# A feed forward with 64-wide inner products: two batches side by side in TensorE's array

## The chip, the cores and the metric

The kernel runs on one core of a Trainium2 chip, in one launch, all in fp32. The metric is the device time of that launch in microseconds (us); "before" is the median of three runs.

## What is computed

The reference is a decoder of four blocks over `x` (4 batches x 256 tokens x 128 features), each an attention over the context and a feed forward, added to `x` through tanh gates. The part that matters here is the feed forward of the second block, a two-layer mixture with low rank R = 64 whose 16 gates come from an entmax:

```python
    def cp_mumoe(x, gate, Win, Wout):
        ones = jnp.ones(x.shape[:-1] + (1,), x.dtype)
        xb = jnp.concatenate([x, ones], axis=-1)
        z = jnp.einsum('btd,dr->btr', xb, Win) * gate
        return jnp.einsum('btr,or->bto', z, Wout)
...
        a = entmax15(layernorm_noaffine(jnp.einsum('btd,de->bte', x, proj)))
        g1 = jnp.einsum('bte,er->btr', a, C1)
        h = cp_mumoe(x, g1, Win1, Wout1)
        h = jax.nn.gelu(h, approximate=False)
        g2 = jnp.einsum('bte,er->btr', a, C2)
        return cp_mumoe(h, g2, Win2, Wout2)
```

Here E = 16 gates, R = 64, D = 128, and the hidden width O = 512. So `C1`, `C2` contract over 16 rows into 64 columns, `Win1` over 128 into 64, `Wout1` over 64 into 512, `Win2` over 512 into 64, and `Wout2` over 64 into 128.

## The kernel before

`x` lies transposed in SBUF, features on the 128 partitions and a batch's 256 tokens along the free dimension. Up to about 1060 us the kernel runs the first block and a long six-layer local attention; then comes `pe_tail`, `act_tail`, `dve_tail` (with small parts in `pool_tail`), which this case is about. Each engine runs its own written-out order of instructions, and semaphores (`s["..."]`) tie them together. In the tail every stage loops over the four batches, and batch b owns the two PSUM banks 2b and 2b + 1 (a bank is 512 fp32 columns per partition).

The stage of this case, by line, is this chain; "product" is one `e.matmul` of the program, which the trace records as two MATMULs:

- Layer norm of `x`: `pe_ln_centre` (L234), square (L239), `pe_ln_var` (L244), Ln and Exp (L249, L251), multiply (L256).
- Router logits (L1289), keys and values of the next attention (L1294, L1296), `Win1` for the four batches (L1301). `IDLE1` = 6 products of 512 columns whose result nobody reads (L1304) keep PE running while DVE computes the entmax (L1615 to L1678).
- `m1_a`: eight transposes turn the gates (L1309), two for each batch.
- Per batch: ACT copies the turned gates (L1517), PE multiplies them by `C1` and `C2` (L1315, L1316), ACT copies both results (L1520), DVE forms `z1` = (Win1 x + bin1) * g1 (L1727).
- Per batch: four products with `Wout1` (L1322), contraction over 64 partitions, 128 columns wide; then two Gelus of 128x512 on ACT (L1523, L1524).
- Per batch: four products with `Win2` accumulate into 64 partitions (L1329); DVE forms `z2` (L1732); `Wout2` (L1335); DVE adds to `x` (L1736).
- The next block begins with the layer norm of `x` (L234 again), then its attention (L1127 and on).

All loops above run over the four batches inside each step, so PE does `Wout1` for all four, then `Win2` for all four, and so on. ACT loads an activation table when the function changes: at L1523 for Gelu by itself, and at L1525, where the program asks for the next one (`preload_act_table_set`).

Other products of the kernel use only a part of the array too: in the fourth block's attention, L1423 contracts over 32 partitions (`rows = slice(32 * (2 * pair + c), ...)`, with c as the innermost loop) and L1437 writes 32 partitions (`out[32 * g:32 * g + 32, :]`, with g as the innermost loop).

Of the kernel before, what the change touches and what calls it, by code (L numbers as in the profile page):

```python
# [10 lines left out]
ALU = mybir.AluOpType  # L11
ACT = mybir.ActivationFunctionType
AX = mybir.AxisListType

B, N, D = 4, 256, 128
P = 128
NT = N // P
BANK = 512
# [10 lines left out]
E1, R1, O1 = 16, 64, 512  # L29
# [45 lines left out]
def split(ap, n):  # L75
    return ap.rearrange("p (n k) -> p n k", n=n)
# [1120 lines left out]
        e.tensor_tensor(p, p, stretch(over, N), ALU.mult).then_inc(s["at_normalised"], 1)  # L1197


HT2_ROWS = [min(P, (E2 + 1) * HID2 - i * P) for i in range(HT2)]  # L1200


# [65 lines left out]
def pe_tail(e, s, m):  # L1268
# [7 lines left out]
    for b in range(B):  # L1276
# [3 lines left out]
                 skip_group_check=True).then_inc(s["mix_made"], 1)  # L1280
# [5 lines left out]
    for b in range(B):  # L1286
        e.wait_ge(s["ln_out"], LN_L1F + b + 1)
        for t in range(NT):
            made = e.matmul(m.bank[2 * b][:, t * E1:(t + 1) * E1], m.xn[b][:, t * P:(t + 1) * P], m.W(7, "proj"),  # L1289
                            start=True, stop=True, skip_group_check=True)  # L1290
        made.then_inc(s["m1_logits"], 1)
    for b in range(B):
        b1 = m.bank[2 * b + 1]
        e.matmul(b1[:, 0:N], m.W(7, "Wk"), m.ctx[b], start=True, stop=True, skip_group_check=True)  # L1294
        for t in range(NT):
            made = e.matmul(b1[:, N + t * P:N + (t + 1) * P], m.ctx[b][:, t * P:(t + 1) * P], m.W(7, "Wv"), start=True,  # L1296
                            stop=True, skip_group_check=True)
        made.then_inc(s["p_made"], 1)
    for b in range(B):
        e.wait_ge(s["p_kept_act"], 8 + b + 1)  # L1300
        e.matmul(m.bank[2 * b + 1][0:R1, 0:N], m.W(7, "Win1"), m.xn[b], start=True, stop=True, skip_group_check=True)  # L1301
    e.wait_ge(s["m1_var"], 1)
    for n in range(IDLE1):
        e.matmul(m.bank[0], m.ident, m.x_all[:, 0:BANK], start=True, stop=True, skip_group_check=True)  # L1304
    e.wait_ge(s["m1_a"], 1)
    for b in range(B):
        for t in range(NT):
            i = b * NT + t
            made = e.transpose(m.bank[2 * b][0:E1, t * P:(t + 1) * P], m.router[7][:, i * E1:(i + 1) * E1], m.ident)  # L1309
        made.then_inc(s["m1_turned"], 1)  # L1310
    for b in range(B):
        b0 = m.bank[2 * b]
        aT = m.t_w[b][0:E1, 0:N]
        e.wait_ge(s["m1_a_kept"], b + 1)
        e.matmul(b0[0:R1, 0:N], m.W(7, "C1")[0:E1, :], aT, start=True, stop=True, skip_group_check=True)  # L1315
        e.matmul(b0[0:R1, N:2 * N], m.W(7, "C2")[0:E1, :], aT, start=True, stop=True,  # L1316
                 skip_group_check=True).then_inc(s["m1_made"], 1)
    for b in range(B):
        z1 = m.t_w[b][0:R1, 2 * BANK:2 * BANK + N]
        e.wait_ge(s["m1_z1"], b + 1)  # L1320
        for o in range(4):
            made = e.matmul(m.bank[2 * b + o // 2][:, o % 2 * N:(o % 2 + 1) * N], m.W(7, "Wout1")[0:R1, o * P:(o + 1) * P],  # L1322
                            z1, start=True, stop=True, skip_group_check=True)
        made.then_inc(s["m1_h"], 1)
    for b in range(B):
        hT = split(m.t_v[b], 4)
        e.wait_ge(s["m1_gelu"], b + 1)
        for o in range(4):
            made = e.matmul(m.bank[2 * b][0:R1, 0:N], m.W(7, "Win2")[:, o * R1:(o + 1) * R1], hT[:, o, :], start=(o == 0),  # L1329
                            stop=(o == 3), skip_group_check=True)  # L1330
        made.then_inc(s["m1_w2"], 1)
    for b in range(B):
        z2 = m.t_w[b][0:R1, 2 * BANK + N:3 * BANK]
        e.wait_ge(s["m1_z2"], b + 1)
        e.matmul(m.bank[2 * b + 1][:, 0:N], m.W(7, "Wout2")[0:R1, :], z2, start=True, stop=True,  # L1335
                 skip_group_check=True).then_inc(s["m1_out"], 1)

    for b in range(B):
        e.wait_ge(s["l1f_done"], b + 1)
# [21 lines left out]
    for step in range(HT2 + LAG2 + 1):  # L1361
        i = step
# [123 lines left out]
def act_tail(e, s, m):  # L1486
# [25 lines left out]
    e.activation(root, delta, ACT.Ln, bias=m.floor).then_inc(s["m1_root"], 1)  # L1512
    e.wait_ge(s["m1_root"], 1)
    e.activation(root, root, ACT.Exp, scale=0.5).then_inc(s["m1_root"], 1)
    for b in range(B):
        e.wait_ge(s["m1_turned"], b + 1)
        e.activation(m.t_w[b][0:E1, 0:N], m.bank[2 * b][0:E1, 0:N], ACT.Copy).then_inc(s["m1_a_kept"], 1)  # L1517
    for b in range(B):
        e.wait_ge(s["m1_made"], b + 1)
        e.activation(m.t_w[b][0:R1, BANK:2 * BANK], m.bank[2 * b][0:R1, :], ACT.Copy).then_inc(s["m1_g"], 1)  # L1520
    for b in range(B):
        e.wait_ge(s["m1_h"], b + 1)
        e.activation(m.t_v[b][:, 0:BANK], m.bank[2 * b][:, :], ACT.Gelu)  # L1523
        e.activation(m.t_v[b][:, BANK:2 * BANK], m.bank[2 * b + 1][:, :], ACT.Gelu).then_inc(s["m1_gelu"], 1)  # L1524
    e.preload_act_table_set("natural_log_exp_and_others")  # L1525
    act_ln4(e, s, m, LN_L2X, m.ln_tail, m.eps)
    act_attention(e, s, m, 2)
# [161 lines left out]
def dve_tail(e, s, m):  # L1689
# [31 lines left out]
    e.wait_ge(s["l1x_done"], B)  # L1721
    dve_ln4(e, s, m, LN_L1F, m.ln_tail, m.xn)
    dve_entmax(e, s, m, link)
    for b in range(B):
        g, z1 = m.t_w[b][0:R1, BANK:2 * BANK], m.t_w[b][0:R1, 2 * BANK:2 * BANK + N]
        e.wait_ge(s["m1_g"], b + 1)
        e.scalar_tensor_tensor(out=z1, in0=m.bank[2 * b + 1][0:R1, 0:N], scalar=m.W(7, "bin1")[0:R1, :], in1=g[:, 0:N],  # L1727
                               op0=ALU.add, op1=ALU.mult).then_inc(s["m1_z1"], 1)
    for b in range(B):
        g, z2 = m.t_w[b][0:R1, BANK:2 * BANK], m.t_w[b][0:R1, 2 * BANK + N:3 * BANK]  # L1730
        e.wait_ge(s["m1_w2"], b + 1)
        e.scalar_tensor_tensor(out=z2, in0=m.bank[2 * b][0:R1, 0:N], scalar=m.W(7, "bin2")[0:R1, :], in1=g[:, N:2 * N],  # L1732
                               op0=ALU.add, op1=ALU.mult).then_inc(s["m1_z2"], 1)
    for b in range(B):
        e.wait_ge(s["m1_out"], b + 1)
        e.scalar_tensor_tensor(out=m.x[b], in0=m.bank[2 * b + 1][:, 0:N], scalar=m.gates[:, B + 1:B + 2], in1=m.x[b],  # L1736
# [286 lines left out]
def chunked(a, rows=P):  # L2023

    n = -(-a.shape[0] // rows)
    full = np.zeros((n * rows,) + a.shape[1:], a.dtype)
    full[:a.shape[0]] = a
    return full.reshape(n, rows, -1).transpose(1, 0, 2).reshape(rows, -1)


def column(a):
    return chunked(a.reshape(-1, 1))
# [6 lines left out]
def layouts(i):  # L2039
# [11 lines left out]
    for d in range(DEPTH):  # L2051
        qs, ks = i["L0_ffn_q_scale"][d], i["L0_ffn_k_scale"][d]
        swap = lambda a: np.concatenate([a[DH // 2:], a[:DH // 2]])
        b1 = i["L0_ffn_b1"][d]
        wqkv = i["L0_ffn_Wqkv"][d]
        wv = wqkv[:, 2 * INNER:].reshape(D, H0, DH)[:, v_order].reshape(D, INNER)
        wo = i["L0_ffn_Wo"][d].reshape(H0, DH, D)[np.array(o_order)].reshape(INNER, D)
        packs.append(packed(L0F, {
            "Wqkv": np.concatenate([wqkv[:, :2 * INNER], wv], 1), "Wo": chunked(wo), "W1": i["L0_ffn_W1"][d],
            "W2": chunked(i["L0_ffn_W2"][d]), "scales": row(np.concatenate([qs, ks, swap(qs), swap(ks)])),  # L2060
            "ln_g": column(i["L0_ffn_ln_g"][d]), "ln_b": column(i["L0_ffn_ln_b"][d]),
            "b1": np.concatenate([column(b1[:FF]), column(b1[FF:])], 1), "b2": column(i["L0_ffn_b2"][d])}))
    one = {}
    for n in ("q_c", "k_s", "v_s", "q_s", "k_c", "v_c"):
        one["W" + n], one["b" + n] = i[f"L1_xattn_W{n}"].T, column(i[f"L1_xattn_b{n}"])
    wg = i["L1_xattn_Wg"].T
    one.update({
        "Wg_a": wg[:D], "Wg_b": wg[D:], "bg": column(i["L1_xattn_bg"]), "proj": i["L1_ffn_proj"],
        "C1": i["L1_ffn_C1"], "C2": i["L1_ffn_C2"], "Win1": i["L1_ffn_Win1"][:D], "bin1": i["L1_ffn_Win1"][D:].T,
        "Wout1": i["L1_ffn_Wout1"].T, "Win2": chunked(i["L1_ffn_Win2"][:O1]), "bin2": i["L1_ffn_Win2"][O1:].T,  # L2070
        "Wout2": i["L1_ffn_Wout2"].T, "gamma": column(i["L2_xattn_gamma"]), "beta": column(i["L2_xattn_beta"])})
    for n in "qkv":
        one["W" + n], one["b" + n] = i["L2_xattn_W" + n], column(i["L2_xattn_b" + n])
    packs.append(packed(MIX1, one))
# [40 lines left out]
```

## Time and profile before

| | us |
|---|---|
| before, median of 3 runs | 1402.86 (1399.28 to 1403.01) |
| the profiled execution, its own time | 1402.63 |
| its span (first to last instruction) | 1400.8 |
| TensorE busy in the span | 1272.3 (91%) |
| VectorE / ScalarE / GpSimdE busy | 980.5 / 934.2 / 741.9 |
| mean granted TensorE clock | 0.963 of full |

The profile is of one execution, and all instants below are microseconds from its span's start. PE is TensorE's matmuls, PEld its weight loads, DVE VectorE, ACT ScalarE, POOL GpSimdE. In a group of rows merged over time, the first number is the start and the second the busy time of the merged instructions. PEclk is the share of TensorE's full clock that was granted: 1.00 is 2.4 GHz, 0.50 is 1.2 GHz. A matmul's duration runs from its start to the end of its last result, so that following matmuls overlap it; the step from one start to the next is what a stream of them costs.

### The profile page before, as it was taken

The numbers are of one execution on the slowest core, as the hardware profiler recorded it, in microseconds if no ns is written. First come the engines' busy times: TensorE is split into PE (matmuls) and PEld (weight loads), VectorE is DVE, ScalarE is ACT, GpSimd is POOL, SyncE is SP. The second block draws the span as 40 slices with busy tenths as digits, with TensorE's granted clock in tenths as the row PEclk, the third lists the DMA queues.
The fourth block names the chain that finished last, engine by engine and source line by source line (L and its number), as shares of the span: only waits on it lengthen the run. The fifth ranks groups of instructions, "written<-read, shape, count | busy, mean of one in ns | idle before, by whom it ended". The sixth has DMA issues, their size and how long they took to land. (4 is left out here: it accounts for less than half of the span.)

```text
span 1400.8 us, 44886 instructions
## 1 busy us (share of the span) xinstructions
PE 1272.3 (91%) x17964; PEld 908.1 (65%) x17964; DVE 980.5 (70%) x2443; ACT 934.2 (67%) x2301; POOL 741.9 (53%) x749
## 2 busy tenths in 40 slices
PE   6999978999999999999999999999878898998767
PEld 4777635667776677677667676767657566775443
DVE  3666658888887888788778888888635524554657
ACT  5777745677776777777677777777546545644971
POOL 3444438887887787878687878777510001002100
PEclk9999989999999999999999999999889978999998
DMA  4000033222234223322332233223102000000000
GB/s 195 1 1 1 1 117 71 68 65 57 66 77 118 63 60 102 96 65 62 94 94 63 62 100 99 63 59 85 43 2 98 1 0 26 1 0 1 1 1 16
DMA packets 68319, 76.95 MB, mean 55 GB/s; under 512 B 14864, under 2 KB 62992, under 8 KB 67600
## 3 DMA queue, kind: packets, MB, share of 16 engines
q1 hardware_dynamic: 68112, 74.07, 19.9%
q8 instruction: 144, 2.36, 0.7%
q14 instruction: 63, 0.52, 0.1%
HBM read 26.31 MB, written 0.52 MB: 19 GB/s over the span
## 5 line engine op out<-in xcount | busy, mean ns | idle before, releaser
L1047 POOL TENSOR_TENSOR arena<-arena,small 128x512 f32<-128x512 f32 x96 | 100.1, 1043 | 155.6 <-DVE small L930 155.6
L795 ACT ACTIVATE arena<-banks 128x512 f32<-128x512 f32 x96 | 57.4, 598 | 147.2 <-PE banks L653 146.9
L906 DVE TENSOR_TENSOR arena<-banks,rotary 128x512 f32<-128x512 f32 x192 | 131.7, 686 | 31.6 <-ACT arena L765 18.2
L1022 POOL TENSOR_TENSOR arena<-arena 128x512 f32<-128x512 f32 x96 | 122.6, 1277 | 38.4 <-DVE arena L908 38.4
L702 PE MATMUL banks<-arena 64*64 64x32 f32 x6144 | 114.3, 222 | 18.7 <-issue 10.5
L1027 POOL TENSOR_TENSOR arena<-arena 128x512 f32<-128x512 f32 x96 | 122.6, 1277 | 2.1 <-DVE arena L908 2.1
L702 PEld LDWEIGHTS banks<-arena 64*64 64x64 f32 x6144 | 101.8, 136 | 29.3 <-ACT arena L817 12.5
L503 POOL TENSOR_TENSOR arena<-arena,small 128x512 f32<-128x512 f32 x64 | 66.5, 1040 | 87.0 <-DVE small L437 87.0
L616 PE MATMUL banks<-slot,z 128*128 128x512 f32 x192 | 102.5, 616 | 6.9 <-DVE z L996 3.4
L717 PE MATMUL banks<-arena,slot 128*128 128x128 f32 x768 | 106.0, 282 | 2.1 <-ACT arena L825 1.9
L1034 POOL TENSOR_TENSOR arena<-arena,small 128x512 f32<-128x512 f32 x96 | 100.4, 1046 | 1.4 <-ACT small L805 1.4
L1053 POOL TENSOR_TENSOR arena<-arena,small 128x512 f32<-128x512 f32 x96 | 100.0, 1042 | 0.9 <-DVE small L938 0.9
L636 PE MATMUL banks<-slot,z 128*128 128x512 f32 x192 | 100.5, 606 | 0.0
L1041 POOL TENSOR_TENSOR arena<-arena,small 128x512 f32<-128x512 f32 x96 | 100.0, 1042 | 0.0
L625 PE MATMUL banks<-slot,z 128*128 128x512 f32 x192 | 99.5, 600 | 0.3 <-DVE arena L908 0.3
L717 PEld LDWEIGHTS banks<-arena,slot 128*128 128x128 f32 x768 | 95.2, 195 | 3.7 <-ACT arena L825 3.1
L645 PEld LDWEIGHTS banks<-constants,arena 128*128 128x128 f32 x384 | 44.0, 145 | 73.2 <-issue 73.1
L947 DVE TENSOR_TENSOR z<-z,banks 64x128 f32<-64x128 f32 x96 | 26.6, 277 | 92.1 <-PE banks L717 92.1
L383 ACT ACTIVATE arena<-arena,small 128x256 f32<-128x256 f32 x128 | 63.7, 500 | 39.8 <-DVE small L466 39.8
L675 PE MATMUL banks<-arena 64*32 64x64 f32 x6144 | 83.6, 225 | 1.0 <-DVE arena L971 0.5
L675 PEld LDWEIGHTS banks<-arena 64*32 64x32 f32 x6144 | 68.2, 106 | 18.6 <-issue 18.5
L908 DVE TENSOR_TENSOR arena<-banks,rotary 128x256 f32<-128x256 f32 x192 | 79.6, 414 | 0.0
(311 smaller groups left out, 3341.0 us busy)
## 6 DMA issues: line engine op xcount, KB each, us to landing
arena<-arena SPq DMA_DIRECT2D x576, 64.0 KB
slot<-in_pack_dram SPq DMA_DIRECT2D x28, 339.5 KB
arena<-arena SPq DMA_DIRECT2D x288, 32.0 KB
slot<-in_pack_dram SPq DMA_DIRECT2D x2, 2713.5 KB
slot<-in_pack_dram SPq DMA_DIRECT2D x1, 3333.0 KB
slot<-in_pack_dram SPq DMA_DIRECT2D x1, 2316.5 KB
slot<-in_pack_dram SPq DMA_DIRECT2D x4, 337.0 KB
slot<-in_pack_dram SPq DMA_DIRECT2D x7, 158.0 KB
```

The lines of the kernel that those rows point to most:

```text
L616: e.matmul(m.bank[QB], m.zs[b][:, t * P:(t + 1) * P], m.W(stage, "Wqkv")[:, half * BANK:(half + 1) * BANK], start=True, stop=True, skip_gr ...
L636: e.matmul(m.bank[VB], m.zs[b][:, t * P:(t + 1) * P], m.W(stage, "Wqkv")[:, at:at + BANK], start=True, stop=True, skip_group_check=True).t ...
L675: made = e.matmul(m.bank[S0 + z][i * WINDOW:(i + 1) * WINDOW, r * SPAN:(r + 1) * SPAN], qT[rows, r, i * WINDOW:(i + 1) * WINDOW], kT[rows, ...
L702: made = e.matmul(m.bank[PB if x else VB][y * DH:(y + 1) * DH, to:to + WINDOW], v[rows, i, k, :], pT[rows, at:at + WINDOW], start=True, st ...
L717: made = e.matmul(m.bank[S0][:, N:N + P], wo[:, c * D:(c + 1) * D], oT[:, k * P:(k + 1) * P], start=(k == 0), stop=(k == UP - 1), skip_gro ...
L906: e.tensor_tensor(rot, made, cos, ALU.mult)
L1022: e.tensor_tensor(m.rot_q[u % ROTS], m.rot_q[u % ROTS], m.sin_q[u % 2], ALU.add).then_inc(s["q_added"], 1)
L1027: e.tensor_tensor(m.rot_k[u % ROTS], m.rot_k[u % ROTS], m.sin_k[u % 2], ALU.add).then_inc(s["k_added"], 1)
L1034: e.tensor_tensor(q, q, stretch(m.local_small[u % 4][:, 0:UH], DH), ALU.mult).then_inc(s["q_rotated"], 1)
L1041: e.tensor_tensor(k, k, stretch(m.local_small[u % 4][:, UH:2 * UH], DH), ALU.mult).then_inc(s["k_rotated"], 1)
L1047: e.tensor_tensor(p, p, stretch(m.local_small[u % 4][:, 16:24], SPAN), ALU.subtract).then_inc(s["lowered"], 1)
L1053: e.tensor_tensor(p, p, stretch(m.local_small[u % 4][:, 32:40], SPAN), ALU.mult).then_inc(s["normalised"], 1)
```

## The change

Batches 2p and 2p + 1 form a pair (p = 0, 1). Where a product fills only 64 partitions of its result (`Win1`, `C1`, `C2`, `Win2`), the first batch of the pair takes partitions 0 to 63 and the second 64 to 127 of the same bank. Where a product contracts over 64 partitions (`Wout1`, `Wout2`), the first batch reads partitions 0 to 63 and the second 64 to 127, into banks of their own; for this the packed weights `Wout1`, `Wout2`, `bin1`, `bin2` are stored twice, one copy above the other. The two products of a pair follow each other directly. The number of products stays the same. ACT's copies and DVE's `z1` and `z2` treat a pair in one instruction; the eight Gelus remain, now in the order half by half of a pair, each with its own semaphore step; the Gelu table is asked for before the copies of the gates. The results of `C1` and `C2` go to bank 4p + 2.

```diff
+def gates1_turned(m, pair):
+    return m.t_w[2 * pair][0:E1, 0:BANK]
+
+def gates1(m, pair):
+    return m.t_w[2 * pair][:, BANK:2 * BANK]
+
+def hidden1(m, pair):
+    return m.t_w[2 * pair][:, 2 * BANK:2 * BANK + N], m.t_w[2 * pair][:, 2 * BANK + N:3 * BANK]
...
-    for b in range(B):
-        e.wait_ge(s["p_kept_act"], 8 + b + 1)
-        e.matmul(m.bank[2 * b + 1][0:R1, 0:N], m.W(7, "Win1"), m.xn[b], start=True, stop=True, skip_group_check=True)
+    for pair in range(2):
+        e.wait_ge(s["p_kept_act"], 8 + 2 * pair + 1)
+        for h in range(2):
+            e.matmul(m.bank[4 * pair + 1][R1 * h:R1 * (h + 1), 0:N], m.W(7, "Win1"), m.xn[2 * pair + h], start=True, stop=True,
+                     skip_group_check=True)
...
+    for pair in range(2):
+        for i in range(2 * NT):
+            at = (2 * NT * pair + i) * E1
+            made = e.transpose(m.bank[4 * pair][0:E1, i * P:(i + 1) * P], m.router[7][:, at:at + E1], m.ident)
         made.then_inc(s["m1_turned"], 1)
...
+    for pair in range(2):
+        aT = gates1_turned(m, pair)
+        e.wait_ge(s["m1_a_kept"], pair + 1)
+        for c in range(2):
+            for h in range(2):
+                made = e.matmul(m.bank[4 * pair + 2][R1 * h:R1 * (h + 1), c * N:(c + 1) * N], m.W(7, ("C1", "C2")[c])[0:E1, :],
+                                aT[:, h * N:(h + 1) * N], start=True, stop=True, skip_group_check=True)
+        made.then_inc(s["m1_made"], 1)
+    for pair in range(2):
+        z1 = hidden1(m, pair)[0]
+        e.wait_ge(s["m1_z1"], pair + 1)
         for o in range(4):
-            made = e.matmul(m.bank[2 * b + o // 2][:, o % 2 * N:(o % 2 + 1) * N], m.W(7, "Wout1")[0:R1, o * P:(o + 1) * P],
-                            z1, start=True, stop=True, skip_group_check=True)
-        made.then_inc(s["m1_h"], 1)
+            for h in range(2):
+                rows = slice(R1 * h, R1 * (h + 1))
+                made = e.matmul(m.bank[4 * pair + 2 * h + o // 2][:, o % 2 * N:(o % 2 + 1) * N],
+                                m.W(7, "Wout1")[rows, o * P:(o + 1) * P], z1[rows, :], start=True, stop=True,
+                                skip_group_check=True)
+                if o % 2:
+                    made.then_inc(s["m1_h"], 1)
+    for pair in range(2):
+        for half in range(2):
+            e.wait_ge(s["m1_gelu"], 4 * pair + 2 * half + 2)
+            for o in range(2 * half, 2 * half + 2):
+                for h in range(2):
+                    made = e.matmul(m.bank[4 * pair][R1 * h:R1 * (h + 1), 0:N], m.W(7, "Win2")[:, o * R1:(o + 1) * R1],
+                                    m.t_v[2 * pair + h][:, o * N:(o + 1) * N], start=(o == 0), stop=(o == 3),
+                                    skip_group_check=True)
         made.then_inc(s["m1_w2"], 1)
+    for pair in range(2):
+        z2 = hidden1(m, pair)[1]
+        e.wait_ge(s["m1_z2"], pair + 1)
+        for h in range(2):
+            rows = slice(R1 * h, R1 * (h + 1))
+            e.matmul(m.bank[4 * pair + 2 * h + 1][:, 0:N], m.W(7, "Wout2")[rows, :], z2[rows, :], start=True, stop=True,
+                     skip_group_check=True).then_inc(s["m1_out"], 1)
...
+    e.preload_act_table_set("gelu_and_others")
+    for pair in range(2):
+        e.wait_ge(s["m1_turned"], pair + 1)
+        e.activation(gates1_turned(m, pair), m.bank[4 * pair][0:E1, :], ACT.Copy).then_inc(s["m1_a_kept"], 1)
+    for pair in range(2):
+        e.wait_ge(s["m1_made"], pair + 1)
+        e.activation(gates1(m, pair), m.bank[4 * pair + 2], ACT.Copy).then_inc(s["m1_g"], 1)
+    for pair in range(2):
+        for half in range(2):
+            for h in range(2):
+                b = 2 * pair + h
+                e.wait_ge(s["m1_h"], 4 * pair + 2 * half + h + 1)
+                e.activation(m.t_v[b][:, half * BANK:(half + 1) * BANK], m.bank[2 * b + half],
+                             ACT.Gelu).then_inc(s["m1_gelu"], 1)
...
+    for pair in range(2):
+        e.wait_ge(s["m1_g"], pair + 1)
+        e.scalar_tensor_tensor(out=hidden1(m, pair)[0], in0=m.bank[4 * pair + 1][:, 0:N], scalar=m.W(7, "bin1"),
+                               in1=gates1(m, pair)[:, 0:N], op0=ALU.add, op1=ALU.mult).then_inc(s["m1_z1"], 1)
+    for pair in range(2):
+        e.wait_ge(s["m1_w2"], pair + 1)
+        e.scalar_tensor_tensor(out=hidden1(m, pair)[1], in0=m.bank[4 * pair][:, 0:N], scalar=m.W(7, "bin2"),
+                               in1=gates1(m, pair)[:, N:2 * N], op0=ALU.add, op1=ALU.mult).then_inc(s["m1_z2"], 1)
...
+    twice = lambda a: np.concatenate([a, a], 0)
```

## Rows read from the trace of the kernel before

**Rows 1.** The page, parts 1 and 2: TensorE's busy share and clock in 40 slices.
```profile
PE 1272.3 (91%) x17964; PEld 908.1 (65%) x17964; DVE 980.5 (70%) x2443; ACT 934.2 (67%) x2301; POOL 741.9 (53%) x749
...
PEclk9999989999999999999999999999889978999998
```
**Rows 2.** The chain that ended last, 1112 to 1160 us (start, us, what).
```profile
1118.47 0.30 DVE small L1678
...
1118.82 1.04 PE banks L1309 x8
...
1124.78 13.95 PE banks L1322 x32
1138.73 8.91 PE banks L1329 x32
1147.63 1.92 PE banks L1335 x8
1149.56 1.92 PE banks L234 x8
```
**Rows 3.** Stretches: length, busy PE, PEld, DVE, ACT, POOL; PEclk; DMA share, GB/s.
```profile
1098.40:1101.40 3.00, 3.00 (x7) 2.46 (x8) 1.11 (x3) 0.83 (x3) 0.00 (x0) 0.50 0.00 0
1101.60:1103.00 1.40, 1.40 (x8) 1.25 (x7) 0.00 (x0) 1.11 (x4) 0.00 (x0) 1.00 0.00 0
1119.80:1121.90 2.10, 2.10 (x11) 1.35 (x11) 0.38 (x1) 1.33 (x5) 0.00 (x0) 1.00 0.00 0
1122.00:1124.70 2.70, 2.70 (x7) 1.13 (x5) 0.95 (x2) 0.94 (x2) 0.00 (x0) 0.50 0.00 0
1124.70:1138.60 13.90, 13.90 (x33) 10.50 (x32) 0.48 (x1) 5.13 (x8) 0.00 (x0) 0.50 0.00 0
1138.60:1142.40 3.80, 3.80 (x10) 2.12 (x10) 0.03 (x1) 2.37 (x3) 0.00 (x0) 0.50 0.00 0
1142.50:1147.50 5.00, 5.00 (x24) 3.02 (x22) 1.29 (x3) 0.00 (x0) 0.00 (x0) 1.00 0.00 0
```
**Rows 4.** Who waited for whom, 1118 to 1151 us.
```profile
DVE arena L1732 <- PE banks L1329: 20.3, 4, 16.5
...
ACT arena L1523 <- PE banks L1322: 8.8, 4, 2.3
```
**Rows 5.** Instructions in order of time, 1120 to 1160 us.
```profile
1120.90 0.59 ACT L1520 ACTIVATE arena<-banks 64x512 f32<-64x512 f32 x1 [0.49 <-PE banks L1316]
1121.52 0.47 DVE L1727 SCALAR_TENSOR_TENSOR arena<-banks,slot,arena 64x256 f32<-64x256 f32 x1 [2.76 <-ACT arena L1520]
1124.71 14.02 PE L1322 MATMUL banks<-arena,slot 64*128 64x256 f32 x32
1125.42 1.28 ACT L1523 ACT_TABLE_LOAD   x1
1128.52 0.60 ACT L1523 ACTIVATE arena<-banks 128x512 f32<-128x512 f32 x1 [1.82 <-PE banks L1322]
1129.02 0.59 ACT L1524 ACTIVATE arena<-banks 128x512 f32<-128x512 f32 x1
1145.95 0.48 DVE L1732 SCALAR_TENSOR_TENSOR arena<-banks,slot,arena 64x256 f32<-64x256 f32 x1 [1.25 <-PE banks L1329]
1147.67 0.47 DVE L1732 SCALAR_TENSOR_TENSOR arena<-banks,slot,arena 64x256 f32<-64x256 f32 x1 [1.25 <-PE banks L1329]
1148.30 1.78 DVE L1736 SCALAR_TENSOR_TENSOR x<-banks,gate_columns,x 128x256 f32<-128x256 f32 x4 [0.15 <-PE banks L1335]
```
**Rows 6.** TensorE's matmuls in order of time, 1300 to 1312 us.
```profile
1301.72 1.07 PE L1437 MATMUL banks<-arena 128*32 128x256 f32 x16 [1.68 <-DVE arena L1821]
1302.72 1.82 PE L1423 MATMUL banks<-arena 32*128 32x256 f32 x16
```
**Rows 7.** Loads' durations: groups by line, 1110 to 1151 us.
```profile
L1322 PEld LDWEIGHTS banks<-arena,slot 64*128 64x128 f32 x32 | 10.5, 332 | 3.6 <-DVE arena L1727 0.8
```

More of the change, by code:

```diff
@@ L1305, in pe_tail @@
     e.wait_ge(s["m1_a"], 1)
[L1306 to L1309, printed above, removed]
+    for pair in range(2):
+        for i in range(2 * NT):
+            at = (2 * NT * pair + i) * E1
+            made = e.transpose(m.bank[4 * pair][0:E1, i * P:(i + 1) * P], m.router[7][:, at:at + E1], m.ident)
         made.then_inc(s["m1_turned"], 1)
[L1311 to L1317, printed above, removed]
@@ L1318, in pe_tail @@
-    for b in range(B):
-        z1 = m.t_w[b][0:R1, 2 * BANK:2 * BANK + N]
-        e.wait_ge(s["m1_z1"], b + 1)
-        for o in range(4):
-            made = e.matmul(m.bank[2 * b + o // 2][:, o % 2 * N:(o % 2 + 1) * N], m.W(7, "Wout1")[0:R1, o * P:(o + 1) * P],
-                            z1, start=True, stop=True, skip_group_check=True)
-        made.then_inc(s["m1_h"], 1)
[L1325 to L1330, printed above, removed]
-        made.then_inc(s["m1_w2"], 1)
@@ L1332, in pe_tail @@
[L1332 to L1336, printed above, removed]
+    for pair in range(2):
[6 more added lines that the diff above has]
+        made.then_inc(s["m1_made"], 1)
@@ L1514, in act_tail @@
     e.activation(root, root, ACT.Exp, scale=0.5).then_inc(s["m1_root"], 1)
[L1515 to L1524, printed above, removed]
+    e.preload_act_table_set("gelu_and_others")
[12 more added lines that the diff above has]
+                             ACT.Gelu).then_inc(s["m1_gelu"], 1)
     e.preload_act_table_set("natural_log_exp_and_others")
@@ L1723, in dve_tail @@
     dve_entmax(e, s, m, link)
[L1724 to L1733, printed above, removed]
+    for pair in range(2):
[6 more added lines that the diff above has]
+                               in1=gates1(m, pair)[:, N:2 * N], op0=ALU.add, op1=ALU.mult).then_inc(s["m1_z2"], 1)
     for b in range(B):
@@ L2068, in layouts @@
         "Wg_a": wg[:D], "Wg_b": wg[D:], "bg": column(i["L1_xattn_bg"]), "proj": i["L1_ffn_proj"],
-        "C1": i["L1_ffn_C1"], "C2": i["L1_ffn_C2"], "Win1": i["L1_ffn_Win1"][:D], "bin1": i["L1_ffn_Win1"][D:].T,
-        "Wout1": i["L1_ffn_Wout1"].T, "Win2": chunked(i["L1_ffn_Win2"][:O1]), "bin2": i["L1_ffn_Win2"][O1:].T,
-        "Wout2": i["L1_ffn_Wout2"].T, "gamma": column(i["L2_xattn_gamma"]), "beta": column(i["L2_xattn_beta"])})
+        "C1": i["L1_ffn_C1"], "C2": i["L1_ffn_C2"], "Win1": i["L1_ffn_Win1"][:D], "bin1": twice(i["L1_ffn_Win1"][D:].T),
+        "Wout1": twice(i["L1_ffn_Wout1"].T), "Win2": chunked(i["L1_ffn_Win2"][:O1]), "bin2": twice(i["L1_ffn_Win2"][O1:].T),
+        "Wout2": twice(i["L1_ffn_Wout2"].T), "gamma": column(i["L2_xattn_gamma"]), "beta": column(i["L2_xattn_beta"])})
     for n in "qkv":
```

## The prediction

> **What bounds the kernel now.** I read the page first: TensorE is busy for 91% of the span, and its clock is below full in some slices, among them those between 1050 and 1200 us [rows 1]. Next the chain that ended last, cut to this stage. From the first transposes at 1118.82 to the end of the next layer norm's L234 at 1151.48 it lies on PE without a break: 13.95 us in `Wout1` (L1322), 8.91 in `Win2` (L1329), 1.92 in `Wout2` (L1335) [rows 2]. The waits say the same from the other side: DVE's `z2` waited 20.3 us in all for L1329, and the Gelus 8.8 us for L1322; the longest wait of a Gelu is 2.3 us, so ACT has room beside PE [rows 4]. So PE's time in this stage is kernel time, nearly one for one, until another engine takes its place.
>
> The third view is the stretches with their clock [rows 3]. PE is busy without a gap from 1119.8 to 1147.5. The clock is 1.00 up to 1121.9 and 0.50 from 1122.0 to 1142.4, through all of L1322 and the first 3.8 us of L1329; then it is 1.00 again. So L1322's 32 matmuls cost 13.95/32 = 0.436 us each, and L1329's last ones (1147.67 - 1145.95)/8 = 0.216 us [rows 2, 5]. I call the step from one start to the next a slot: about 0.427 at the low clock and 0.216 at the high one.
>
> **Do two halves of the array run at once?** The number of products is unchanged, so everything hangs on this. Sixteen matmuls of 256 columns in slots of 0.216 would take 3.4 us one behind the other, or 3.6 with the last one's tail. L1437, in four column groups of 32, does 16 in 1.07 us; L1423, with two row groups of 32 in turn, does 16 in 1.82 us, both with loads between them [rows 6]. That is four abreast and two abreast with next to nothing lost. The changed products have the same pattern: halves in the innermost loop, row halves into different banks as L1423, column halves into one bank as L1437. Only their size, 64, is not shown with 256 columns. I take two abreast in full, with one product each as the other end.
>
> The Trainium skill speaks less favourably of packing: its page "TensorE: Matmul & The Clock Gate", section "Measured speedup vs the span model", has 3.07x for four row tiles. Scaled to two that would be an estimate of some 1.5x instead of 2x, and would take back about 2.5 us of the sum below. The rows above give 2x for two row groups, and they decide.
>
> **The change part by part**, at the instants of this execution.
>
> *Up to `z1`.* Nothing before `m1_a` gets later: `Win1` gets 0.5 to 0.8 us shorter, but DVE's entmax ends at 1118.77 whatever PE does [rows 2]. Four transposes instead of two stand before the first copy: eight take 1.04, four 0.64, so 1119.46. The copy is now 16x512; I take 0.59 from the 64x512 one (L1520) [rows 5], and PE goes on at 1120.10. `C1` and `C2` for a pair are 8 matmuls in 4 slots, at the high clock 0.27 + 2 x 0.216 + 0.37 = 1.07 to the end: 1121.21 with the signal. The copy is 128x512 instead of 64x512, and I take 0.59 again, since its free size is the same and L1524's 128x512 took 0.59; `z1` takes 0.47 [rows 5]. `Wout1` begins at 1122.36, where before it began at 1124.71: 2.35 us gained. The Gelu table (1.28 us, at 1125.42 before [rows 5]) moves into ACT's wait before the transposes (about 1116.2 to 1119.4), so it is free; without that cover up to 1.28 us would fall before the first copy.
>
> *`Wout1`.* 32 matmuls in 16 slots. What is the clock? It fell at 1122 behind the 16-row products, which are as light after the change, so I let it fall at the same instant. Alone, 64-row products did not bring it back in 13.9 us of unbroken work. Full-height ones did: on 128x128 products from 1098.4 it was 0.50 and from 1101.6 it was 1.00, and it came back at 1142.4 after 3.8 us of 128x64 [rows 3]. Two row halves abreast fill the array as a full product does, so I expect it back after about 3 us of L1322, near 1125.4. Then 7 slots are low and 9 high: 7 x 0.427 + 9 x 0.216 = 4.93, plus 0.07 for the first: 5.0 us in place of 13.95, so 8.95 gained.
>
> *Gelus.* The first two can begin at 1124.5. They follow each other at 0.50 us (1128.52, 1129.02 [rows 5]), 4 us for eight, behind PE: the last half is made at about 1127.9, the last Gelu ends at 1129.0, and `Win2` needs it at about 1130.0. So ACT is covered by about 1 us. If the clock never were low, ACT would set the pace here.
>
> *`Win2`.* 32 matmuls in 16 slots at the high clock, 3.45 us plus 0.05 for the change of shape, in place of 8.91: 5.4 gained; PE is through at about 1130.9.
>
> *`z2`, `Wout2`, `x`.* Before, 3.85 us passed from the end of L1329 to the end of L234 [rows 2]. Now: 0.15 tail, `z2` 0.47, `Wout2`'s pair 0.70, then the additions of the pair, 0.48 + 0.43 (L1736: 1.78 for four [rows 5]), and L234 for the last batch 0.70, with signals 3.15. The first pair's additions run beside it. Gained 0.7.
>
> Sum: 2.35 + 8.95 + 5.4 + 0.7 = 17.4 us. What follows (layer norm, attention) is the same work and merely starts earlier; no load from HBM is near its due time there. Where the clock changes is not fixed to the work, so I hold two neighbouring cases against it: back one low stretch later, so that 15 of `Wout1`'s 16 slots are low, 15.7 us; never low, with ACT's Gelus as the pace, 18.9 us. I take 17.0.
>
> The same page of the Trainium skill, section "What's actually happening", says that sustained activity of the array releases the clock. This trace disagrees as far as busy time goes: PE was busy 13.90 of 13.90 us in L1322 and stayed at 0.50. By the page alone the clock would not be low in this stage at all, which is the 18.9 case.
>
> **The rivals.**
> - *The clock stays low through the paired `Wout1` as it did through the single one* and rises only in `Win2`, after some 3 us of it. For it: a 64-row product never raised it here. Against: L1423 and L1437 ran packed at the high clock. `Wout1` then ends at 1129.3 and `Win2` at 1134.2, a gain of 14.1: 1388.5.
> - *The clock does not fall at all*, since the 16-row products are over sooner and full ones follow: 18.9, so 1383.7.
> - *Row halves overlap but 64-column halves do not.* `Win2` then keeps 32 slots (+3.45) and `C1`/`C2` eight (+0.86): a gain of 13.1, 1389.5. Against it stands L1437.
> - *The change does not do what it says:* no two products overlap. `Wout1` and `Win2` cost what they cost, only copies and `z` shrink, which are hidden, and the 16x512 copy adds 0.2: 1402 to 1403.
> - *Slower:* no overlap, and each switch of halves also exposes the load that now lies under the previous matmul. For `Wout1` that is 32 x 0.332 = 10.6 us [rows 7], for `Win2` and the rest some 8 more: 1421. It decides as soon as a pair takes more than two slots (0.86 us at the low clock). L1423 and L1437 switch groups at every product and show nothing of it [rows 6].
>
> **How the numbers follow.** The sum is made against the profiled execution, 1402.63 us of its own with a span of 1400.8; the median of the runs is 1402.86, so the two agree. 1402.63 - 17.0 = 1385.6. Chances: this forecast 0.62, clock low for longer 0.15, clock never low 0.12, columns not abreast 0.05, no overlap 0.04, slower 0.02. The runs of before lie 3.7 us apart (1399.28 to 1403.01), about what one or two low stretches elsewhere cost; so around 1385.6 I put 4 us below, and above I reach past the two partial cases: 1381.5 to 1391.0. About 0.3% (4.2 us) is what a measurement of this kernel tells from no change; every case but the last two is beyond it, so faster 0.94, same 0.04, slower 0.02.
>
> **What would show it.** In the profile after: `Wout1`'s 32 matmuls within 5 to 7 us instead of 14.0, `Win2`'s within 3.5 to 4; their starts in twos; the clock 1.00 again before `Win2` begins; DVE's longest wait for `Win2` near 6.5 us instead of 16.5; the table load before the copies; from the first transpose to the end of L234 about 15.2 us instead of 32.7. The forecast is wrong if `Wout1` still takes 14 us (no overlap), if it takes 6.8 at 0.50 and the clock stays there (the first rival), or if the next stage runs longer at 0.50 than before, which would give part of the gain back.

## The result and the profile after

| | before | changed |
|---|---|---|
| first comparison, median of 6 runs each | 1398.68 us (1395.14 to 1403.01) | 1380.92 us (1377.70 to 1387.64) |
| ratio, 95% interval | | 0.9869 (0.9834 to 0.9904) |
| second comparison (`e2_changed`), medians of 17 and 6 runs | 1404.73 us | 1381.14 us (1377.52 to 1385.54) |
| ratio, 95% interval | | 0.9839 (0.9811 to 0.9867) |

The kernel is faster by 1.3 to 1.6%. The forecast was 1385.6 us in a range of 1381.5 to 1391.0; the median lies 0.6 us below that range. The direction and the mechanism were right; what was off, as worked out below, is the level from which the gain was subtracted, and its spread.

The chain that ended last, in the profile of the changed kernel, from the last step of the entmax to the next stage (start, us, what). It answers to [rows 2].

```profile
1112.01 0.30 DVE small L1705
...
1112.36 0.62 PE banks L1323 x4
1113.00 0.59 ACT arena L1541
...
1113.64 1.10 PE banks L1330 x8
1114.76 0.61 ACT arena L1544
1115.39 0.49 DVE arena L1753
...
1115.93 5.24 PE banks L1339 x32
1121.17 3.60 PE banks L1349 x32
1124.77 1.29 PE banks L1358 x8
1126.06 1.92 PE banks L234 x8
```

L1323 are the gate transposes, L1330 `C1` and `C2`, L1339 `Wout1`, L1349 `Win2`, L1358 `Wout2`. `Wout1` takes 5.24 us for its 32 matmuls where it took 13.95, `Win2` 3.60 where it took 8.91. From the first transpose (1112.36) to the end of L234 (1127.98) the chain is 15.6 us long; before it was 32.7 (1118.82 to 1151.48). I call this distance "the stage" from here on. That the chain now passes once through ACT's and DVE's copies before `Wout1` is the price of pairing: PE stands still for them, and still gains.

The stretches of the changed kernel, with the same columns as [rows 3]; they end at the changes of the clock.

```profile
1112.30:1115.60 3.30, 2.98 (x24) 1.66 (x24) 0.21 (x1) 1.66 (x3) 0.00 (x0) 1.00 0.00 0
1115.70:1119.00 3.30, 3.07 (x14) 2.54 (x16) 0.66 (x2) 1.48 (x3) 0.00 (x0) 0.50 0.00 0
1119.10:1121.00 1.90, 1.90 (x20) 1.49 (x16) 0.00 (x0) 1.55 (x5) 0.00 (x0) 1.00 0.00 0
1121.10:1124.70 3.60, 3.60 (x34) 2.21 (x32) 0.48 (x1) 2.70 (x4) 0.00 (x0) 1.00 0.00 0
```

The clock falls behind the 16-row products as before, but it is back after 3.1 us of paired `Wout1`; single 64-row products ran 13.9 us at 0.50 without bringing it back [rows 3]. By the mean clock of the stage, given below, that is about 3.5 us at 0.50 (15.7 x 2 x 0.11) instead of about 20 (32.7 x 2 x 0.31).

The waits of the changed kernel, 1112 to 1128 us, answer to [rows 4].

```profile
DVE arena L1757 <- PE banks L1349: 7.6, 2, 6.4
...
ACT arena L1550 <- PE banks L1339: 2.2, 2, 1.8
...
PEld banks L1349 <- ACT arena L1550: 0.3, 1, 0.3
```

DVE's longest wait for `Win2` is 6.4 us where it was 16.5. The last line, of `Win2`'s first weight load, must be read with care. It names the Gelu whose signal came last, but the program lets `Win2` begin after the first two Gelus.

ACT in order of time, in the same profile, shows the moved table load (at L1538) in the gap ahead of the transposes, and the eight Gelus (L1550) at 0.50 us each.

```profile
1109.72 1.28 ACT L1538 ACT_TABLE_LOAD   x1
1113.00 1.06 ACT L1541 ACTIVATE arena<-banks 16x512 f32<-16x512 f32 x2 [1.99 <-PE banks L1323]
...
1119.47 3.04 ACT L1550 ACTIVATE arena<-banks 128x512 f32<-128x512 f32 x6 [0.35 <-PE banks L1339]
```

The first two Gelus end at 1119.12 (1118.04 + 1.08), 2 us before `Win2` begins; the last ends at 1122.51 (1119.47 + 3.04), and PE reaches the products that need it at 1123.74. So the Gelus stay ahead of PE by 1.2 us or more, and hold nothing up.

One number does not fit: the spans differ by 23.1 us (1400.8 and 1377.7), the stage by 17.0. The whole execution cut in five, first before, then changed: up to the stage, the stage, up to the fourth block's attention, that attention, the rest.

```profile
0.00:1118.80 1118.80, 1035.10 (x16700) 746.68 (x16700) 832.74 (x2104) 781.83 (x1813) 723.37 (x728) 0.98 0.25 67
1118.80:1151.50 32.70, 32.68 (x105) 22.02 (x106) 5.58 (x12) 11.58 (x21) 0.00 (x0) 0.69 0.00 0
1151.50:1289.70 138.20, 126.19 (x540) 93.19 (x539) 69.75 (x173) 71.72 (x186) 6.88 (x9) 0.94 0.02 7
1289.70:1359.30 69.60, 46.70 (x514) 27.99 (x513) 44.22 (x65) 61.26 (x261) 11.61 (x13) 0.94 0.01 1
1359.30:1400.80 41.50, 31.65 (x112) 18.19 (x112) 28.20 (x89) 7.78 (x20) 0.00 (x0) 0.87 0.05 13
```

```profile
0.00:1112.30 1112.30, 1029.70 (x16700) 743.00 (x16700) 831.96 (x2104) 783.05 (x1814) 723.38 (x728) 0.98 0.26 68
1112.30:1128.00 15.70, 15.05 (x105) 10.31 (x106) 3.59 (x8) 8.82 (x16) 0.00 (x0) 0.89 0.00 0
1128.00:1266.20 138.20, 126.10 (x536) 93.16 (x535) 69.75 (x173) 71.71 (x186) 6.83 (x9) 0.94 0.02 7
1266.20:1335.80 69.60, 46.71 (x514) 28.07 (x513) 44.20 (x65) 61.26 (x261) 11.67 (x13) 0.94 0.00 1
1335.80:1377.70 41.90, 31.69 (x112) 18.21 (x112) 28.19 (x89) 7.78 (x20) 0.00 (x0) 0.87 0.05 13
```

Behind the stage the two are alike within 0.4 us. The other 6.5 us lie ahead of it, where both kernels run the same program up to the last few products. Is that luck of the execution, or does the change do it? And is the gain two abreast, the clock, or the shared copies?

### The profile page after: what moved, and what is told of

Read it like the earlier page. It is cut to its first block and busy times, and to the rows that moved or that the text cites. A ratio compares the mean times of both kernels' runs of the same rounds, so it can differ in the third digit from the quotient of the medians.

```text
span 1377.7 us, 44878 instructions
## 1 busy us (share of the span) xinstructions
PE 1249.3 (91%) x17964; PEld 892.8 (65%) x17964; DVE 977.7 (71%) x2439; ACT 932.6 (68%) x2297; POOL 741.9 (54%) x749
## 5 line engine op out<-in xcount | busy, mean ns | idle before, releaser
L616 PE MATMUL banks<-slot,z 128*128 128x512 f32 x192 | 101.1, 608 | 6.9 <-DVE arena L908 3.6
L636 PE MATMUL banks<-slot,z 128*128 128x512 f32 x192 | 98.5, 595 | 0.0
L625 PE MATMUL banks<-slot,z 128*128 128x512 f32 x192 | 98.0, 592 | 0.0
L645 PEld LDWEIGHTS banks<-constants,arena 128*128 128x128 f32 x384 | 42.8, 142 | 72.7 <-issue 72.0
L686 PEld LDWEIGHTS banks<-constants,arena 128*128 128x128 f32 x384 | 47.6, 142 | 50.7 <-issue 30.0
```

The source lines that it names most:

```text
L616: e.matmul(m.bank[QB], m.zs[b][:, t * P:(t + 1) * P], m.W(stage, "Wqkv")[:, half * BANK:(half + 1) * BANK], start=True, stop=True, skip_gr ...
L636: e.matmul(m.bank[VB], m.zs[b][:, t * P:(t + 1) * P], m.W(stage, "Wqkv")[:, at:at + BANK], start=True, stop=True, skip_group_check=True).t ...
```

## Experiments

Three theories were in play. A: two products abreast, with the clock that comes back through them, make the stage 17 us shorter, and the rest is run-to-run. B: the change gains ahead of the stage too. C, later sharpened to D: the fourth attention's time depends on when it starts. Ratios are to the kernel before, run alongside. The runs were made in four sets, each on a chip of its own (`e1` to `e4`, `e5` to `e8`, `e9` to `e11`, `e12`), so across sets the ratios are safer to compare than the medians. The ratios are not ratios of the medians, and differ from them by up to 0.24%.

### e1_null and e2_changed: both kernels again, unedited

> The kernel before, unchanged, against itself. Theory A: the two profiles differ by 23.1 us in span, of which 17.0 lie in the stage (first gate transpose to the end of the next L234: 32.7 against 15.6 us) and 6.5 before it, where the program is the same (first transpose at 1118.8 against 1112.4); that part is run-to-run, from where the low-clock stretches fall. Then the ratio is 1.000 within 0.3%, single runs spread over some 8 us, and this profile has its first transpose anywhere between 1111 and 1120 with a stage of 31 to 34 us. Theory B: the changed kernel is also faster ahead of the stage; then this kernel's first transpose stays at 1118 to 1120.

> The changed kernel, unchanged, for a second set of runs and a second profile. Theory A: ratio 0.987 to 0.989 (16 to 18 us), stage 14 to 18 us, first transpose anywhere between 1111 and 1120. Theory B: ratio 0.983 to 0.985 (21 to 24 us), first transpose again near 1112.4.

The null comparison gave 1405.72 us (1396.39 to 1419.05, 12 runs), ratio 1.0014 (0.9990 to 1.0038). The changed kernel gave the second line of the table at the top. The first transpose came at 1115.2 in `e1_null` and at 1111.0 in `e2_changed`; over all runs of this study it lay between 1109.8 and 1118.8 with no order by kernel (1109.8 in a form of the kernel before, 1118.8 in the kernel before itself). So the 6.5 us were the execution's, and theory B falls. The first profile of before, with 1118.8, is the longest of all fourteen ahead of the stage; the other thirteen lie at 1115.7 or below. The stages were 31.0 and 15.8 us. But the profile of `e1_null` has another slow part (the same five stretches, columns as above):

```profile
1146.20:1284.30 138.10, 126.06 (x541) 93.40 (x539) 69.77 (x173) 71.72 (x186) 6.88 (x9) 0.94 0.02 7
1284.30:1365.90 81.60, 57.09 (x514) 30.59 (x513) 43.80 (x65) 61.49 (x261) 11.61 (x13) 0.70 0.00 1
```

The fourth attention took 81.6 us at a mean clock of 0.70, with the same 514 matmuls that took 69.6 us at 0.94 in the first profile. One and the same kernel can differ by 12 us in this part alone.

### e3_serial and e4_rows_serial: the halves of a pair one after the other

```diff
-        for o in range(4):
-            for h in range(2):
+        for h in range(2):
+            for o in range(4):
                 made = e.matmul(m.bank[4 * pair + 2 * h + o // 2][:, o % 2 * N:(o % 2 + 1) * N],
```

(`e4_rows_serial` has this for `Wout1` alone, `e3_serial` also for `C1`/`C2` and `Win2`; the Gelus follow in the same order.)

> The changed kernel with its halves, banks and shared copies, but the products of one batch of a pair all before those of the other (batch outside, columns inside), for C1/C2, Wout1 and Win2. Theory A (two abreast and the clock that comes back with it make the gain): Wout1 about 13 to 14 us at 0.50, Win2 6 to 9 us, stage 27 to 31 us, ratio 0.996 to 1.000. Rival (the shared copies and z, the earlier Gelu table and the earlier start make it): stage under 22 us, ratio under 0.992.

> Only Wout1 one batch after the other, Win2 and C1/C2 still two abreast. Theory A: Wout1 13 to 14 us at the low clock (64-row products alone do not bring it back), Win2 about 4 to 6 us (it starts low, rises within), stage 24 to 27 us, ratio about 0.994 to 0.996. Rival (the clock would have come back anyway because the products of C1/C2 end sooner): Wout1 about 7 to 9 us, stage 19 to 21 us, ratio about 0.990.

Both expectations missed: stages of 18.0 and 18.4 us, not 27 to 31 and 24 to 27. Ratios 0.9908 (0.9876 to 0.9940) and 0.9918 (0.9895 to 0.9942). The groups and stretches of `e3_serial` say why (the group's columns: busy, mean ns of one, idle before it; the stretches lie within `Wout1`):

```profile
L1339 PE MATMUL banks<-arena,slot 64*128 64x256 f32 x32 | 6.5, 508 | 0.3 <-DVE arena L1753 0.3
```

```profile
1118.30:1119.20 0.90, 0.86 (x4) 0.78 (x5) 0.48 (x1) 0.35 (x1) 0.00 (x0) 1.00 0.00 0
1119.30:1122.60 3.30, 3.30 (x16) 3.04 (x15) 0.00 (x0) 1.68 (x3) 0.00 (x0) 0.50 0.00 0
1122.70:1124.80 2.10, 2.10 (x16) 1.64 (x12) 0.00 (x0) 1.80 (x4) 0.00 (x0) 1.00 0.00 0
```

Sixteen matmuls run within 3.3 us at 0.50. One behind the other they would need 16 x 0.427 = 6.8 us. So products of the second half run beside those of the first although PE's program has them eight matmuls apart: the later half of one batch overlaps the earlier half of the next. For the stage the order within a pair matters only a little, 2.2 to 2.8 us; as a test of the first theory the two runs decide nothing. The halves had to be put further apart. The medians are 11 to 12 us above the changed kernel's in the same set, more than the stages explain: the profile of `e4_rows_serial` has its fourth attention at 81.8 us, while that of `e3_serial` is of the fastest of its six runs and has it at 69.7.

### e5_all_apart and e6_rows_apart: first batches of both pairs, then second batches

```diff
-    for pair in range(2):
-        z1 = hidden1(m, pair)[0]
-        e.wait_ge(s["m1_z1"], pair + 1)
-        for o in range(4):
-            for h in range(2):
+    for h in range(2):
+        for pair in range(2):
+            z1 = hidden1(m, pair)[0]
+            e.wait_ge(s["m1_z1"], pair + 1)
+            for o in range(4):
```

> The changed kernel with everything shared as it is, but with all products of the first batches of both pairs ahead of all products of the second ones, in C1/C2, Wout1 and Win2, so that hardly two different halves stand near each other in PE's order. Theory A: nothing overlaps then: Wout1 12 to 14 us, at 0.50 throughout, Win2 6 to 8.5 us, stage 28 to 31 us, time within 3 us of the kernel before. Rival (what the copies and z share makes a good part): stage under 26 us.

> Only Wout1 with the two halves that far apart; C1/C2 and Win2 two abreast. Theory A (64-row products alone keep the clock low): Wout1 12 to 13.5 us, mostly at 0.50, Win2 4 to 6 us, stage 24 to 27 us, 8 to 11 us slower than the changed kernel. Rival (the clock comes back by itself after the lighter C1/C2): Wout1 8 to 9 us, stage near 20 us, 4 to 5 us slower.

`e5_all_apart`: 1407.79 us (1395.91 to 1411.85), ratio 1.0010 (0.9976 to 1.0043); its stage takes 28.7 us. `e6_rows_apart`: 1399.39 us (1387.74 to 1404.09), ratio 0.9969 (0.9942 to 0.9995); stage 25.0 us. Both stages fell into theory A's bounds. The medians are 3.6 us above the kernel before (by its ratio `e5_all_apart` can't be told from it) and, against another set, 18 above the changed one. Both are more than expected, and the profiles have their fourth attention at 85.5 and 80.5 us. The stretches of `e6_rows_apart` (`Wout1`, then `Win2` up to the clock's return, then its rest):

```profile
1114.20:1126.80 12.60, 12.46 (x34) 9.57 (x35) 0.56 (x2) 4.50 (x8) 0.00 (x0) 0.50 0.00 0
1126.80:1131.10 4.30, 4.30 (x23) 2.40 (x24) 0.48 (x1) 1.88 (x2) 0.00 (x0) 0.50 0.00 0
1131.20:1132.60 1.40, 1.40 (x16) 0.71 (x12) 0.00 (x0) 0.00 (x0) 0.00 (x0) 1.00 0.00 0
```

With the same halves, banks, copies and number of products, `Wout1` alone is 12.5 us at 0.50 when its halves don't meet, and the clock returns only in `Win2`. That is 7.2 us more in `Wout1` and 2.2 in `Win2` than in the changed kernel. So the gain of the stage splits like this, in this order of undoing: pairing of `Wout1` with its clock 9.4 us (25.0 - 15.6), pairing of `C1`/`C2` and `Win2` 3.7 (28.7 - 25.0), and the shared copies, `z` and the remaining overlap at the border 2.3 to 4.0 (31.0 to 32.7 before, less 28.7). No run parts the overlap from the clock inside the 9.4 us. By an estimate, paired `Wout1` with all 16 slots at 0.50 would take 16 x 0.427 + 0.07 = 6.9 us, so some 5.5 us are the overlap, and 1.7 in `Wout1` and 2.2 in `Win2` the clock.

### e7_idle8 and e8_shift: unread products more

```diff
-IDLE1 = 6
+IDLE1 = 8
```

```diff
                      skip_group_check=True).then_inc(s["m1_out"], 1)
+    for n in range(2):
+        e.matmul(m.bank[6], m.ident, m.ctx_all[:, 0:BANK], start=True, stop=True, skip_group_check=True)
```

> The changed kernel with 8 instead of 6 products that nobody reads ahead of the gate transposes, so that PE waits 0.1 instead of 1.8 us before them. Theory A (the fall of the clock in the stage comes from the light 16-row products alone): one low stretch stays, stage 15.5 to 16, time as the changed kernel within 2 us. Rival (the wait ahead of the transposes has its part): no low stretch in the stage, which takes 14 to 14.5 us, 1 to 1.5 us faster.

> The changed kernel with two more unread products (512 columns each, 1.7 us on PE) between Wout2 and the next layer norm, which start everything later by 1.7 us. Theory A (the gain beyond the 17 us of the stage is a matter of where low stretches happen to fall, run by run, and not tied to when the later stages start): median 1 to 3.5 us above the changed kernel. Theory C (it is tied to the start of the later stages against the clock's steps, which run by themselves): median off by 5 us or more, or lower.

`e7_idle8` still has its low stretch in the stage, which takes 15.6 us. PE's wait ahead of the transposes is gone (1.8 us in the changed kernel) and the fall behind the 16-row products stays, so that wait has no part in it. Yet the median is 1389.49 us (1377.30 to 1394.73), 8 us above the changed kernel in another set. The ratio, 0.9891 (0.9851 to 0.9931), overlaps both of the changed kernel's, so this surplus is not clear of noise. `e8_shift` gave 1392.01 us (1384.86 to 1398.16), 10.9 above it for 1.7 us of work; its ratio, 0.9914 (0.9885 to 0.9943), is clear of the second comparison's and overlaps the first's. Both profiles have a long fourth attention: 75.9 us at a mean clock of 0.79, and in `e8_shift`

```profile
1265.00:1350.40 85.40, 60.31 (x514) 31.00 (x513) 43.62 (x65) 61.72 (x261) 11.62 (x13) 0.63 0.00 1
```

It isn't the only part that moves. Between the stage and the fourth attention `e8_shift` took 134.7 us at a mean clock of 0.97, the profile of `e2_changed` 141.4 at 0.92, so `e8_shift` won back 6.7 of the 16.2 us that its attention cost.

### e9_changed_filled, e10_before_filled, e11_before_shift, e12_filled_no_preload

```diff
         if n >= LAG3 and (n - LAG3) % 2:
+            if n < UNITS3 - 1:
+                e.wait_ge(s["s3_exped"], n - 1)
+                e.matmul(m.bank[2 * ((n + 1) % 3)], m.ident, m.x_all[:, 0:BANK], start=True, stop=True, skip_group_check=True)
```

(An unread product in PE's waits within the fourth attention, 14 in all and not the 15 of the expectation. `e11_before_shift` is the edit of `e8_shift` on the kernel before; `e12_filled_no_preload` is `e9_changed_filled` without the early request for the Gelu table.)

> The changed kernel with one unread product of 512 columns (0.86 us on PE) in each of PE's waits for the values of the fourth attention (15 of them, waits of 1.1 to 1.7 us). Theory D (the rest of the difference between before and after, and the spread of each, is that attention: 69 us where the clock stays up, 76 to 85 where it falls into long low stretches, and which of the two depends on where its start lies against the clock's steps): the attention takes 68 to 71 us in the profile with under 10 us at 0.50, the twelve runs lie within 9 us, median 1377 to 1382. Rival (the fillers delay PE or the long stretches have another cause): attention 75 us or more, median above 1385.

> The kernel before with the same fillers. Theory D: attention 68 to 71 us, median 1394 to 1399, that is 6 to 9 us below the plain kernel before, and 15 to 18 us above the changed kernel with fillers, which is the stage alone. Rival (the change gains 20 us and more by itself, wherever): still 20 us or more above the changed kernel with fillers.

> The kernel before with two more unread products (1.7 us) between Wout2 and the next layer norm. Theory D: the median moves by something else than +1.7 us, between -6 and +8, since the start of the fourth attention lies elsewhere against the clock's steps; the profile's attention takes either 69 to 70 us with under 11 us at 0.50, or 76 to 86 with over 30. Theory A (no such tie): +1 to +3 us.

> The changed kernel with fillers, without the early request for the Gelu table, so that ACT loads it at the first Gelu. By the prediction's step the early load is free, and the late one falls between the second copy of C1/C2 and the first Gelu, where ACT has a gap of 1.8 us for its 1.28: stage within 0.2 us of 15.6, time within 2 us of the changed kernel with fillers. Rival (the load then delays the first Gelu and all behind it): stage 16.3 to 16.9.

| | median, us | lowest to highest | ratio to before | stage | fourth attention |
|---|---|---|---|---|---|
| e9_changed_filled | 1380.08 | 1375.79 to 1382.80 (6) | 0.9856 (0.9822 to 0.9890) | 15.6 | 71.6 |
| e10_before_filled | 1395.85 | 1391.86 to 1399.31 (12) | 0.9978 (0.9956 to 0.9999) | 31.0 | 71.6 |
| e11_before_shift | 1409.67 | 1396.65 to 1414.14 (12) | 1.0053 (1.0021 to 1.0085) | 32.7 with the two products | 84.1 |
| e12_filled_no_preload | 1383.48 | 1382.64 to 1387.94 (6) | 0.9884 (0.9853 to 0.9914, another set of runs) | 15.6 | 71.6 |

The attention of `e10_before_filled`, and below it that of `e11_before_shift`:

```profile
1277.70:1349.30 71.60, 56.74 (x542) 28.53 (x541) 44.18 (x65) 61.59 (x261) 11.65 (x13) 0.97 0.00 1
```

```profile
1282.80:1366.90 84.10, 60.98 (x514) 31.69 (x513) 43.62 (x65) 61.57 (x261) 11.64 (x13) 0.63 0.00 1
```

With the fillers the long form is gone from the profiles, and the mean clock of all 24 filled executions is 0.965 to 0.976; the 23 plain ones of before, in the set of `e9` to `e11`, have 0.948 to 0.970. Each filled kernel's runs lie within 7.5 us of each other (plain before, in the same set: 1391.41 to 1408.64). The medians of `e9` and `e10` differ by 15.8 us, which agrees with the 15.4 us between their stages; the two profiles alone don't show it (spans of 1381.0 and 1390.1), since the parts ahead of the stage and behind it differ by several us the other way.

Theory D has two halves. That the fourth attention can be long at a low clock, and that this widens the spread of the kernel before, is shown. `e10_before_filled` is only 3.1 us below the plain kernel before (1398.91 in that set), not 6 to 9, and the filled attentions take 71.6 us, not 68 to 71. The two unread products move the kernel before by 10.8 us in the median and by 3 to 12 us by the ratio's interval, so by more than their 1.7 us; the expectation had at most 8.

That the start decides which form comes is not shown. Counted from the span's start, the attention began at 1266.2 (the first profile of the changed kernel) and 1268.2 (`e2_changed`) in the short form and between them, at 1267.2 (`e4_rows_serial`), in the long one; `e3_serial` began at 1269.8 and took 69.7 us, `e7_idle8` at 1269.5 and took 75.9. Against the changes of the clock it is no clearer: in both of these the clock first falls 6.4 us after the attention's start, for 3.4 us in `e3_serial` and for 10.2 in `e7_idle8`.

As for the table load, `e12` confirms that either place is free: it lies in ACT's gap before the first Gelu (1118.07 to 1119.35; the Gelu starts at 1119.87), and the stage is the same to 0.1 us. Its median is 3.4 us above `e9`'s where at most 2 were expected; it comes from another set of runs, the intervals of the two ratios overlap, and the profile shows nothing for it.

## Why the prediction was right, and where it was wrong

**Two abreast** was right, and at full rate: 32 matmuls of `Win2` in 3.60 us against 3.45 + 0.05 worked out, where 32 slots would have been 6.9.

**The terms**, predicted and measured: up to `Wout1` 3.54 us after the first transpose and 3.57; `Wout1` 5.0 and 5.24; `Win2` 3.5 and 3.60; from there to the end of L234 3.15 and 3.21. Stage: 15.2 and 15.6; gain 17.4 and 17.0. `Wout1` had 7 low slots and 9 high ones, as worked out; its excess lies at its two ends: the first step took 0.59 us and the one from its last pair to `Win2` 0.31, where 0.50 and 0.22 stood in the sum. ACT's cover, given as about 1 us, was 1.2. That the forecast of 17.0 meets the measured 17.0 exactly is in part luck: the sum gave 17.4, the 17.0 was a weighing against two neighbouring cases, neither of which came about, and the terms ran over by 0.4 us in all.

**The clock** did as forecast: down behind the 16-row products, up again about 3 us into the pairs. `e6_rows_apart` shows that this is the pairs' doing and not that of the shorter stage. The Trainium skill's sentence in "TensorE: Matmul & The Clock Gate", section "What's actually happening", that sustained activity releases the clock, was weighed against the trace of before; in `e6_rows_apart` too PE was busy 12.46 of 12.60 us and stayed at 0.50.

**The rivals**: a clock low for longer, a clock never low, columns that don't overlap, no overlap, exposed loads. None came about in the changed kernel. `e5_all_apart` shows what the fourth would have looked like. No run shows the first, a clock that stays low through products in pairs.

**The step that failed** is the first of "How the numbers follow": "1402.63 - 17.0 = 1385.6", with "4 us below" as the allowance. It took one execution, and the three runs around it, as the level of the kernel before. The other three of its six runs took 1398.08, 1395.14 and 1396.00 us, and the median of all six is 1398.68. Of the 4.7 us between 1385.6 and the measured 1380.92, this level makes 3.95; the other 0.76 are the gain, 17.76 between the medians where 17.0 was forecast. 1398.68 less 17.0 would have been 1381.7.

What made the profiled execution of before a long one is not the fourth attention, which it ran in the short form (69.6 us). It is the stretch ahead of the stage: 1118.8 us, where the thirteen other profiles have 1109.8 to 1115.7. So a level read from one execution carries the luck of at least three parts of the kernel: 9 us ahead of the stage, 134.6 to 141.4 us between the stage and the fourth attention, and 69.2 to 85.5 us in that attention. The one profile of before could not show this, but the kernel's runs in this study lie between 1391.41 and 1419.05 us, and "1399.28 to 1403.01" was taken for their spread. The allowance below was too small for that reason.

"The same work and merely starts earlier" held within 0.4 us in the profiles of the first comparison. It is no rule: in the second comparison the profiles differ by 28.0 us, 15.2 of them in the stage and 12.4 in the fourth attention, and the medians by 23.6.

**Open**: what decides how long the fourth attention takes. It is not one long form but a range (75.9 us at 0.79, 80.5 to 81.8 at 0.70, 84.1 to 85.5 at 0.63). In `e1_null` PE was busy for 57.1 of 81.6 us where it was busy for 46.7 of 69.6 before, so the surplus is nearly all in PE's own work at the lower clock; its idle time is 24.5 us and 22.9. Why the clock stays down there is not shown. Nor is it settled why the plain kernel before had medians of 1398.7, 1404.7, 1404.2, 1398.9 and 1401.4 in five sets of runs; the last four sets ran on four different chips, and a difference between chips is an untested rival.

## What to carry to other kernels

A product that contracts over 64 rows, or fills 64 columns, can be paired with another batch's on the other half of the array at the cost of a second copy of the weights, and the pair was worth more than a factor of two here (`Wout1` 13.95 us and 5.24), where single half-height products left the clock low. The two need not be neighbours in the program: eight recorded matmuls apart they still overlapped for the greater part, sixteen apart hardly. When such a change is judged in a kernel with light, waiting stretches of PE elsewhere, cut both profiles into the same stages and compare stage by stage; a difference in total that no stage's work explains may be a stage whose clock fell, and filling its waits with unread products made the two versions here comparable. The filled changed kernel, at 1380.08 us, is not distinguishable from the plain one at 1381.14, nor is its spread (7.0 us and 8.0, six runs each); what the fillers steadied is the kernel before. And take the level of a kernel from many runs, not from the one that was profiled.

## What the runs showed of the hardware that was not expected

- PE runs products of different halves beside each other even where its program has all eight matmuls of one batch's `Wout1` ahead of the other's: 16 matmuls in 3.3 us at 0.50 (`e3_serial`), twice the rate of one half alone.
- The same 514 matmuls of the fourth attention take 69.2 to 69.7 us or 75.9 to 85.5 us; in the first form the mean clock is 0.93 to 0.94, in the second 0.63 to 0.79. With 14 unread products in its waits (542 matmuls for 514) it takes 71.6 us at a mean clock of 0.97 in the three filled profiles: more work on PE, and a steadier time.
- At 0.50, single 64-row products kept PE busy for 12.5 to 14.0 us without a rise of the clock, in six profiles of five kernels; the same products in pairs had it back after 3.1 us in the first profile of the changed kernel.
